# A fused attention, expert and state-space kernel on one core: spreading keys straight from SBUF, under a newly placed order of calls

## What is computed

```
def step(S, inp):
    Sk = einsum('bhde,bhe->bhd', S, kt)
    S_new = at * S - at * bt * Sk[..., :, None] * kt[..., None, :] + bt * vt[..., :, None] * kt[..., None, :]
    ot = einsum('bhd,bhde->bhe', qt, S_new)
```

## Time and profile before

| | |
|---|---|
| Median of 3 runs | 563.9 us (563.74 to 564.15) |
| The profiled execution | 564.0 us, of which span 561.9 us |
| PE busy | 464.7 us, 83% |
| ACT busy | 392.8 us, 70% |
| DVE busy | 378.4 us, 67% |
| POOL busy | 188.4 us, 34% |
| Mean granted TensorE clock | 0.936 of 2.4 GHz |
| DMA | 36.49 MB, mean 65 GB/s |

### The profile page before, as it was taken

The page is one execution under the profiler, slowest core; times in us unless marked ns, Lnnn a source line. Parts: engine busy times, 40 slices in busy tenths (PEclk is TensorE's granted clock), DMA queues, the critical chain, the costliest instruction groups (busy, mean ns, idle before and its releaser), DMA issues.

```text
span 561.9 us, 6536 instructions
## 1 busy us (share of the span) xinstructions
PE 464.7 (83%) x2110; PEld 312.2 (56%) x2110; DVE 378.4 (67%) x665; ACT 392.8 (70%) x661; POOL 188.4 (34%) x188
## 2 busy tenths in 40 slices
PE   3695696678966978999998989999997998997079
PEld 2584572566744765666675555667664576652023
DVE  1247878898779999789998976999414176111820
ACT  4777867776798548888746997665998757754243
POOL 0243651576145963048970105332002000011001
PEclk9977897879978999899998999999999999998779
DMA  7636793032440311800320081000000000000000
GB/s 195 245 105 171 226 309 97 18 102 69 121 89 1 94 39 58 189 2 1 95 76 0 1 193 37 0 2 0 1 1 20 0 2 0 1 19 0 1 1 19
DMA packets 35761, 36.49 MB, mean 65 GB/s; under 512 B 12936, under 2 KB 30992, under 8 KB 35472
## 3 DMA queue, kind: packets, MB, share of 16 engines
q1 hardware_dynamic: 35440, 31.88, 21.9%
q10 hardware_dynamic: 288, 4.19, 2.0%
HBM read 31.61 MB, written 3.28 MB: 62 GB/s over the span
## 4 chain that ended last, share of the span: by engine, by line
PE 40%; ACT 27%; DVE 19%; issue 9%; POOL 2%; DMA 2%; SPq 1%; DVEq 0%; ACTq 0%; POOLq 0%
PE psF L761 9%; PE psS L779 9%; ACT hid L1325 4%; ACT L1131 4%; ACT L1129 4%; DVE U L1861 3%; DVE T L1863 3%; DVE T L1859 3%; PE psB L718 2%; ACT hS L1174 2%; PE psA L593 2%; PE psM L822 2%; PE psF L836 2%; ACT sq L1159 2%; PE psM L829 1%
## 5 line engine op out<-in xcount | busy, mean ns | idle before, releaser
L779 PEld LDWEIGHTS psS<-we2s,hid 128*128 128x128 f32 x1024 | 137.7, 198 | 61.5 <-issue 42.6
L761 PE MATMUL psF<-h,we1s 128*128 128x512 f32 (+1 forms) x320 | 142.7, 540 | 12.7 <-ACT hid L1325 11.7
L779 PE MATMUL psS<-we2s,hid 128*128 128x128 f32 x1024 | 141.0, 283 | 8.6 <-ACT hid L1325 5.5
L1325 ACT ACTIVATE hid<-psF,col 128x512 f32<-128x512 f32 (+1 forms) x160 | 93.2, 600 | 55.7 <-PE psF L761 54.9
L761 PEld LDWEIGHTS psF<-h,we1s 128*128 128x128 f32 x320 | 56.7, 203 | 42.7 <-ACT hid L1325 21.4
L2253 POOL TENSOR_TENSOR QS<-H,qn 128x512 f32<-128x512 f32 x32 | 49.1, 1548 | 58.0 <-DVE H L1869 58.0
L1882 DVE SCALAR_TENSOR_TENSOR acc<-psS,gate,acc 128x128 f32<-128x128 f32 x128 | 36.1, 341 | 45.5 <-PE psS L779 45.5
L1869 DVE TENSOR_TENSOR_SCAN H<-A,T 128x576 f32<-128x576 f32 x32 | 55.1, 1721 | 1.1
L1131 ACT ACT_TABLE_LOAD x42 | 53.9, 1283 | 1.4 <-PEq L2402 0.7
L1861 DVE TENSOR_REDUCE U<-T 128x64 f32<-128x576 f32 x32 | 38.6, 1205 | 1.1
L1129 ACT ACT_TABLE_LOAD x30 | 38.5, 1283 | 0.5
(11 more groups left out here) (198 smaller groups left out, 777.1 us busy)
## 6 DMA issues: line engine op xcount, KB each, us to landing
wrep<-scratch_dram SPq DMA_DIRECT2D x64, 144.0 KB, 3.5
krep<-scratch_dram SPq DMA_DIRECT2D x64, 128.0 KB, 3.0
hid<-fold_mats_dram SPq DMA_DIRECT2D x22, 256.0 KB, 3.6
we1s<-we_dram ACTq DMA_DIRECT2D x1, 2048.0 KB, 10.1
we2s<-we_dram ACTq DMA_DIRECT2D x1, 2048.0 KB, 17.4
wrep<-XX SPq DMA_DIRECT2D x8, 144.0 KB, 3.6
outT_dram<-x SPq DMA_DIRECT2D x4, 256.0 KB, 2.6
scratch_dram<-XX SPq DMA_DIRECT2D x3, 288.0 KB, 2.1
```

What stands on the lines that cost most here:

```text
L761: mm(bank[name][:, 0:ncols(w)], we1s[:, e, k * P:(k + 1) * P], h2[w % 2][:, 0:ncols(w)], start=True, stop=True).then_inc(s_hid_mm, 1)
L779: last = mm(bank[name][:, t * P:(t + 1) * P], hid[n % 2][:, k, t * P:(t + 1) * P], we2s[:, e, k, :], start=(k == 0), stop=(k == HT - 1))
L1325: nc.scalar.activation(hid[x_ % 2][:, k, 0:c], psF[n % 2][:, 0:c], ACT.Silu, bias=pc("be1", HT * e + k)).then_inc(s_hid_done, 1)
```

## The change

1. **Spreading without a copy in DRAM.** The scratch tensor, the stores into it and the waits on them are gone. Eight transfers per half remain, now one per e: from the 16 source partitions `e::8` of `kn` or `XX`, each read 8 times by a repeating dimension, to all 128 partitions of `krep[:, e, :]`.
2. **Later reuse of `kn` and `XX`.** As these tiles are now the sources, POOL waits in `keys(n)` and at the end of `decay_products(n)` for the transfers of all halves of the window before, where it waited for one store.
3. **Order.** The lists of calls of all five engines are written anew. PE, DVE, POOL and SP make the same calls in another order; the work itself is the same.

```diff
             def spread_keys(w):
-                n = ncols(w)
                 sp.wait_ge(s_kn_done, w + 1)
-                sp.dma_start(scratch[w, 0, :, 0:n], kn[:, 0:n]).then_inc(s_kn_out, 16)
-                sp.wait_ge(s_kn_out, 16 * (w + 1))
                 for i, h in enumerate(halves(w)):
                     if h > 1:
                         sp.wait_ge(s_outer_done, CPH * (h - 1))
-                    for d in range(DH):
-                        sp.dma_start(krep[h % 2][d::DH, :, :], scratch[w, 0, :, i * HC:(i + 1) * HC].rearrange(
-                            "(h e) n -> h e n", e=DH)).then_inc(s_krep_in[h % 2], 16)
+                    for e in range(DH):
+                        sp.dma_start(krep[h % 2][:, e, :], kn[e::DH, i * HC:(i + 1) * HC].unsqueeze(1).broadcast_to(
+                            [HEADS, DH, HC])).then_inc(s_krep_in[h % 2], 16)
...
             def spread_solved(w):
                 sp.wait_ge(s_x_sub, (CH - 1) * (w + 1))
-                sp.dma_start(scratch[w, 1, :, 0:n // CH * C9], XX[:, 1, 0:n // CH, :].rearrange("p g i -> p (g i)")).then_inc(s_xk_out, 16)
-                sp.wait_ge(s_xk_out, 16 * (w + 1))
...
-                    for d in range(DH):
-                        sp.dma_start(wrep[h % 2][d::DH, 0:DH, :], scratch[w, 1, :, i * H9:(i + 1) * H9].rearrange(
-                            "(h e) n -> h e n", e=DH)).then_inc(s_wrep_in[h % 2], 16)
+                    at, end = i * HC // CH, (i + 1) * HC // CH
+                    for e in range(DH):
+                        sp.dma_start(wrep[h % 2][:, e, :], XX[e::DH, 1, at:end, :].rearrange("p g i -> p (g i)").unsqueeze(1).broadcast_to(
+                            [HEADS, DH, H9])).then_inc(s_wrep_in[h % 2], 16)
...
             def decay_products(n):
...
-                if n > 0:
-                    pool.wait_ge(s_xk_out, 16 * n)
+                for h in (halves(n - 1) if n > 0 else ()):
+                    pool.wait_ge(s_wrep_in[h % 2], 16 * DH * (h // 2 + 1))
...
             def keys(n):
...
-                if n > 0:
-                    pool.wait_ge(s_kn_out, 16 * n)
+                for h in (halves(n - 1) if n > 0 else ()):
+                    pool.wait_ge(s_krep_in[h % 2], 16 * DH * (h // 2 + 1))
```

More of the change, by code:

```diff
@@ L915, in _ @@
[L915 to L919, removed]
+            slot(0, 26)
+            slot(0, 27)
+            project(3, 4)
+            slot(0, 28)
+            variance(("moe", 1))
+            router(1)
+            for s in range(29, 32):
+                slot(0, s)
             slot(1, 0)
             slot(1, 1)
-            gate_rows(1)
+            logits(1)
+            center(("front", 4))
             slot(1, 2)
-            center(("front", 4))
@@ L937, in _ @@
+            slot(1, 17)
             key_products(3, 0)
             key_products(3, 1)
-            for s in range(14, 23):
+            slot(1, 18)
+            variance(("front", 4))
+            slot(1, 19)
+            key_products(3, 2)
+            for s in range(20, 24):
                 slot(1, s)
-            key_products(3, 2)
             key_products(3, 3)
-            slot(1, 23)
             attn_out(3)
-            project(4, 0)
+            for i in range(0, 3):
+                project(4, i)
@@ L963, in _ @@
             project(4, 4)
+            slot(2, 3)
             gate_rows(2)
-            slot(2, 3)
             slot(2, 4)
+            slot(2, 5)
+            experts_back(1)
+            slot(2, 6)
+            slot(2, 7)
             router_bias(2)
-            experts_back(1)
-            slot(2, 5)
-            slot(2, 6)
             center(("ssd", 0))
-            for s in range(7, 11):
+            for s in range(8, 11):
                 slot(2, s)
@@ L977, in _ @@
             slot(2, 12)
-            slot(2, 13)
             attn_out(4)
-            for s in range(14, 19):
-                slot(2, s)
-            ssd_in(0)
-            for s in range(19, 23):
+            for s in range(13, 19):
                 slot(2, s)
             key_products(4, 0)
+            slot(2, 19)
+            ssd_in(0)
+            slot(2, 20)
             key_products(4, 1)
+            slot(2, 21)
             attn_out(5)
+            slot(2, 22)
             slot(2, 23)
@@ L1055, in _ @@
-            slot(4, 3)
+            ffn_up(1, 0)
+            ffn_up(1, 1)
+            logits(4)
+            ffn_up(1, 2)
             ffn_up(1, 3)
             ffn_down(1)
+            slot(4, 3)
             slot(4, 4)
@@ L2034, in _ @@
             convolve(1)
+            chunk(0, 0)
+            chunk(0, 1)
+            ln(("front", 2))
+            ssd_halo(0)
+            chunk(0, 2)
+            couple(1, 0)
             carry(2)
-            ln(("front", 2))
-            for i in range(0, 3):
-                chunk(0, i)
-            couple(1, 0)
+            couple(1, 1)
             chunk(0, 3)
-            for i in range(1, 4):
-                couple(1, i)
+            couple(1, 2)
+            couple(1, 3)
             solve(1)
@@ L2290, in _ @@
             attn_residual(0)
+            read_state(1, 0)
             decay_products(2)
-            read_state(1, 0)
+            read_state(1, 1)
             keys(2)
-            for i in range(1, 4):
-                read_state(1, i)
+            read_state(1, 2)
+            read_state(1, 3)
             attn_residual(1)
@@ L2317, in _ @@
             ssd_residual(0)
-            read_state(4, 0)
             ffn_residual(0)
             experts_residual(2)
-            for i in range(1, 7):
+            for i in range(0, 8):
                 read_state(4, i)
             attn_residual(6)
-            read_state(4, 7)
             attn_residual(7)
```

652 lines of the change are left out of this document (321 added, 331 removed).

## The result

The changed kernel takes **568.33 us** (median of 5 runs, 565.77 to 570.26) and the kernel before 563.74 in the same comparison: a ratio of 1.0077, with a 95% interval of 1.0046 to 1.0107. It is slower by 0.8%, and the forecast was 568.0. The profiled execution took 567.62 us with a span of 565.8 (before 564.0 and 561.9), so the pair of traces shows 3.6 to 3.9 us of the 4.6.

A forecast was written before the change was run, and what follows sets the result against it. No engine alone was taken to set the time (PE busy 83%); the start is a chain through all engines. 564.0 + 11 (start) - 3 (earlier solve, copy included) - 4 (table loads) = 568.0 us; likeliest 564 to 573, wider range 559 to 576.

The forecast's parts named there:

- Part 1: At the start, expert weight loads at the head of ACT's list hold up the first matmul: about +11 us.
- Rival A: At the start, small runs go in groups and the hold-up is only +4 us: 561 us, faster; 18%.
- Part 2: In the spreads, dropping the copy in DRAM saves 1.8 us per window, on the chain in two windows.
- D: In the spreads, the repeating source is slow, +10 us on two spreads: 578 us; 5%.
- Part 3: Key products together, solve earlier: about -2 us at the first window, -2.5 more at the second; 3 taken, copy's saving included.
- Part 4: On ACT, 72 table loads instead of 79, 8 fewer up to the last expert: about -4 us.
- The sum: Whole kernel: 564.0 + 11 - 3 - 4 = 568.0 us.
- B: Start held up, but DVE's 8 us and the table loads' 10.3 in part arrive: 563 us, no change; 14%.
- C: The slowest DMA engine sets the start, +14 us, and only 2 come back: 576 us; 13%.
- Part 5: POOL's new waits for the spreads of the window before cost 0 us.

The follow-up runs named there:

- experiment 1: The kernel before, with only the expert weight loads moved to the head of ACT's list: 576.41 us, 1.0204 against the kernel before.
- 3: The changed kernel with the expert weight loads moved from the head of ACT's list to behind the first window's convolution, about 23 us: 557.41 us, 0.9884 against before.
- 4: The changed kernel with each expert weight load, still first on ACT, cut in two, so packets have 1 KB and not 16 KB: 566.54 us.
- 6: The kernel before with only the new spreading without the DRAM copy and POOL's waits that belong to it, in the old order: 563.64 us.
- 7: The changed kernel (new order, weights first) with the old spreading through DRAM and POOL's old waits: 568.16 us.
- 8: The kernel of 3 with the old spreading through DRAM: 557.99 us.
- 9: The kernel of 3 with eight table loads put back, four pairs at expert activations of windows two to four: 564.92 us.
- 2: The changed kernel with the expert weight loads moved from the head of ACT's list to about 64 us: 565.84 us.
- 11: The kernel of 3 with SP taking three maps ahead of the first window's keys and three more ahead of its solved keys: 558.5 us.
- 5: The changed kernel with one weight load (we1s) at the head of ACT's list and the other (we2s) behind the first window's convolution: 564.58 us.
- 10: The kernel before, old order, with only the expert weight loads moved to behind the first window's convolution, about 25 us: 567.41 us.

## Why the prediction was right, step by step

**Part 1, the start: right.** The first matmul was predicted for 16.5 us and stood at 16.18, q10 had 83.8% of the DMA time up to 13 us, and the loads' place alone costs 12.8 us by the medians of experiment 1 (8.6 to 14.4 by the interval) or 10.9 (3 against the changed kernel) where the term was 11. Rival A fell with it: the small packets of `x` and `C` did not go in groups, as while q10's 275 packets went only 274 of q1's did. The Trainium skill's rule ("DMA: Bandwidth & Descriptors", section "Queues, rings and completion order") that a queue's turn is a packet of some 9 to 17 descriptors is not what the traces show: 275 packets against 274 in 13 us, and a start that moved with the size of the other queue's packets (4). The measurement decides. The step left one thing out, SP's own issue, below.

**Part 2, the copy: the piece right, its way to the end not shown.** The solve to the first chunk became 1.92 us shorter where I had 1.78, the transfers are issued in 5.03 us and land after 2.4 and 2.9. D fell. At the end it shows in no median; by the profiles it is worth 1.8 us in the old order and nothing in the new one (6 to 8).

**Part 3, products together: mis-sized.** Its term and part 2's together said that the first slot would come 1.8 us earlier against the start. It came 2.6 us later (13.1 less 10.54), at 107.2 where I had 102 to 105. The second window's chunk came 1.5 us earlier (9.1 late, less 10.54) where I had 8, at 109.5 and not at 101 to 106. The first window's chunk, 67.0, lies at the edge of my 63 to 67, and without part 2 it would be 0.7 later against the start than before. Two causes can be read. First, I moved POOL's products with the start, at 30.3 + 10.5, but the first `kn` stands at 44.01, 3.2 later: PE has more to do ahead of it, as these rows of before, the kernel of 3 and the changed kernel show, from the first matmul to `kn`:

```profile
5.60:30.30 24.70, 15.52 (x71) 12.63 (x71) 4.94 (x18) 17.95 (x35) 4.40 (x10) 0.95 0.69 222
```

```profile
5.60:31.80 26.20, 16.93 (x78) 14.01 (x78) 5.73 (x23) 18.18 (x35) 3.97 (x10) 0.93 0.96 327
```

```profile
16.20:44.00 27.80, 18.56 (x78) 15.31 (x78) 5.82 (x23) 18.11 (x35) 3.95 (x9) 0.94 0.60 190
```

Seven matmuls more are 1.4 us of PE, and the stretch is 1.5 longer. The other 1.6 are the same 78 matmuls taking longer in the changed kernel's profile. The place is the first modulation; the kernel of 3 first, then the changed one, then the kernel of 9:

```profile
18.75 0.70 PE L594 MATMUL psB<-sq,C 128*128 128x256 f32 x2 [2.18 <-ACT sq L1155]
19.29 1.05 PE L629 MATMUL psS<-hf,M 128*128 128x256 f32 x4
```

```profile
29.37 1.22 PE L594 MATMUL psB<-sq,C 128*128 128x256 f32 x2 [2.18 <-ACT sq L1155]
30.38 1.91 PE L629 MATMUL psS<-hf,M 128*128 128x256 f32 x4
```

```profile
18.78 1.22 PE L594 MATMUL psB<-sq,C 128*128 128x256 f32 x2 [2.18 <-ACT sq L1155]
```

The same two matmuls take 1.22 us and not 0.70. It is not the changed kernel's own: the kernel of 9 has the loads in the gap and the same code as that of 3 up to here, and has 1.22 too. In the profiles of 2, 8 and 11 these two take 0.70, but those after them are slow, and the stretch is longer still. The granted clock explains a part. In the profile of 2 it was 0.82 over the stretch, being at the lower of its two levels (1.2 GHz) from about 20 to 30 us. In that of 5 it was 1.00, the upper level (2.4 GHz), and PE was busy for longest, 21.19 us for the same 78 matmuls:

```profile
5.50:34.70 29.20, 19.96 (x78) 17.09 (x78) 5.73 (x23) 18.07 (x35) 3.94 (x9) 0.82 0.60 189
```

```profile
10.80:41.20 30.40, 21.19 (x78) 17.94 (x78) 5.83 (x23) 18.08 (x35) 3.95 (x9) 1.00 0.73 246
```

The cause stays open. The old order has 24.6 to 24.9 us from the first matmul to the first `kn` in four profiles and the new one 26.2 to 30.5 in eight (4 left out, where PE waits for ACT in it). So the new order is later there, by at least 1.3 us; by how much more, these profiles can't tell. Second, the gain that I put at the second window, a wait of DVE for PE, is there in part: 2.67 us became 1.92. I had taken the products' place in PE's list for the time at which they run.

**Part 4, the table loads: mis-sized the other way.** I took 0.42 of each for the end, from the share that the loads have on the chain of the kernel before. Putting eight back cost 7.5 us (9), not 4. The share on one chain counts a load only where the chain happens to run over ACT; that each load also takes away lead that PE uses up later is a likely reason, not a shown one.

**The sum: right because two errors cancel.** Up to the first slot I had +9.2 (11 less 1.8) and it was +13.1; behind it I had -5.2 (the rest of the sum) and it was -9.2. So +3.9 and -4.0: that the time fits to 0.3 us is luck, while the size of part 1 is not. Taken together parts 2 to 4 were worth 6.3 us by the medians of experiment 3, and I had 7. B's mechanism, that the table loads' 10.3 us arrive for the most part, did act, if the loads put back stand for those taken out; it did not decide since the slot came late. C had the start at 14, it was 10.5. Part 5's zero stands: among POOL's waits in the changed kernel there is none for a spread. No experiment took it alone.

**What stays open:** what the copy is worth in the old order, between 0 and 2 us; what the kernel of 10 loses, if it does; why the same early matmuls are quick in one execution and slow in the next; and of the 9.2 us behind the first slot the 1.8 (9.2 less 7.4) that the table loads don't account for.

## What to carry to other kernels

Count the packets ahead of the first small tile, not the bytes: here a load with large packets on another queue held every small one back for as long as it ran, and the delay was its own length. Such a load goes where nothing on the other queues is needed next, and that has to be read anew once the order changes: the same loads at 64 to 66 us held PE up nowhere in one order and cost 8 us in the other. And a share on the chain of waits is no price of an instruction that leads a chain again and again (0.42 by the chain, 0.73 when put back); putting some back in tells more. And a late start of something is put down to an edit only when the stretch that the edit touches has grown: at the first slot 1 to 3 us came and went here in a stretch that no edit touched.

## What the runs showed of the hardware

- The issue of a small DMA can take microseconds while packets wait on its queue. While q10's large packets ran, SP took 3.66 and 4.66 us to issue the transfers of `csil` and `col`; before they took 0.42 and 0.43. In 4, ACT needed 11.11 us for two of its own loads with 1 KB packets, and its next instruction waited for that. That the queue was full is my reading; no view shows it.
- A spread from one SBUF tile into another with a repeating source, 128 KB, lands 2.4 us after its issue, and one through DRAM after 3.0; both are issued at 0.6 us each.
- The same 78 matmuls of the start kept PE busy for 16.9 to 21.2 us in nine profiles. The granted clock does not sort them: 0.93 with 16.93 us (3), 0.82 with 19.96 (2), 1.00 with 21.19 (5).
